# A gathered convolution, two mixtures of experts and attention in one kernel: the gather's start split in two, its edge products in column tiles, and attention's side work moved between the score steps

## The chip, the cores and the metric

The kernel runs on one core of one Trainium2 chip. The metric is the time of one execution on the device in microseconds (us). The kernel before was timed three times, and one further execution was taken with the hardware profiler. Engines are named as the profile names them: PE is TensorE (PEld its weight loads), DVE is VectorE, ACT is ScalarE, POOL is GpSimd, and SP is SyncE, which here only issues DMAs.

## What is computed

The input is 8 sequences of 256 tokens with 128 channels. Two layers follow one another, each a mixing stage and a mixture of 8 experts.

```python
# layer 0, mixing: a convolution whose taps are gathered at computed positions
wave = (x @ wave_w.T + wave_b).reshape(B, L, 8, 2)
freq = 1 + sigmoid(wave[..., 0]) * 15
phase = tanh(wave[..., 1]) * freq
offs = phase[..., None] + freq[..., None] * (arange(32) - 15.5)
pos = clip(arange(L)[None, :, None, None] + offs, 0, L - 1)
gathered = g0 + (pos - floor(pos)) * (g1 - g0)     # rows floor(pos), floor(pos) + 1
kmat = (x @ kernel_w.T).reshape(B, L, 8, 64)       # 64 bins of weights per token and head
w = take_along_axis(kmat, bins(offs), axis=3)
y = einsum('blhs,blhsd->blhd', w, gathered) @ out_w.T
# layer 0, experts: layernorm, top 2 of 8, gelu(x w1 + b1) w2 + b2, then @ expm(g0) expm(g1) expm(g2),
#   mixed with a dense gelu branch through a sigmoid gate
# layer 1, mixing: attention with 16 heads of 8 channels, softmax over 256 keys, then a projection
# layer 1, experts: layernorm, top 2 of 8, (silu(x W1) * (x W2)) W3
```

## The kernel before

It is a hand-ordered program in four stages that end at a barrier each: gather, experts of layer 0, attention, experts of layer 1. In each stage every engine has one list of instructions written out in order, and semaphores carry the data between the lists. An engine takes its instructions strictly in that order, so one that waits holds back all behind it.

**Gather.** The tokens are cut into `NT` = 16 tiles of 128. PE first makes the wave projection of all tiles, from which DVE and ACT make the parameters `par` of every token and head (`FR`, `INV`, `CC`). Each tile then passes through `positions` (ACT, eight activations over 328 grid points), `fractions` (DVE: `whole_tap`, `rest` and the two small pieces of `edge`), `ramps` (ACT), `weighted` (DVE: `rest`, `edge`, `summed`), `turned` and `edges_turned` (PE transposes into `tp_all` and `CF`), `transposed` (ACT copies them to `AT` and `cfS`), `gathered` (PE: products into `yps`, from `AT` with the differenced rows `xn`, and the edge products `YC` from `cfS` with the coarse rows `xc`), `mixed` (ACT, `yS`), `out_rows` (PE) and `output` (ACT). The differenced rows `xn` = `AT` - `xn` are made once, by POOL. The kernels of a tile (`projected` on PE, `kernels` on DVE, two operations on POOL) are stored to DRAM (`store`) and loaded back skewed by nine DMAs (`load`), all issued by SP. The product of three matrix exponentials is a serial chain of 27 steps (`chained` on PE, `chain_step` on DVE), unrelated to the tiles. The first `EARLY` = 4 steps and kernels stand ahead of the tiles, the others are placed between the tiles' operations by `between`:

```python
def step_at(n, place):
    i = EARLY + 3 * n + place - (place > 1)
    return i if place != 1 and i < CHAIN else None
def kernel_at(n, place):
    return n + EARLY if place == 1 and n + EARLY < NT else None
```

So a tile carries three chain steps: one at place 0, which DVE meets in the middle of `fractions(n + 1)` and PE ahead of `turned(n - 1)`, and two at places 2 and 3, close together at the end of `weighted(n)`; PE does the place 3 step just ahead of `gathered(n - 1)`, and the next place 0 step just behind it.

**Attention.** There are 10 rounds for 8 sequences. In round `i`, scores of sequence `i` are made in eight steps of two heads (`scores`: four matmuls into `s_ps`, and in the same step four of the transposed scores `st_ps` of sequence `i - 1`). DVE reduces `s_ps` to row maxima (`largest`, two reductions a step), ACT takes the exponentials of `st_ps` (`powers`, two a step), and the next step on PE waits for both. Everything else is side work between the steps: `project` (PE), `high` (ACT) and `split` (DVE) make queries and keys, `value_rows` the values, `negated` (DVE), `maxima` (PE) and `add_maxima` (DVE) put the maxima into the queries, `values` (PE) and `outputs` (ACT) multiply with the values, `by_token` (PE) and `averaged` (DVE) divide, and two transposes `ot`, a copy `oT` on ACT and two matmuls `pj` on PE project and add to `xs_all` on DVE. The side work shares three PSUM banks `x_ps`. POOL rounds the last stage's weights (two CASTs at L1196, two subtractions at L1200) beside round 0.

## Time and profile before

| | us |
|---|---|
| median of 3 runs | 907.07 (905.65 to 907.98) |
| the profiled execution's own time | 901.43 |
| its span | 899.6 |
| busy: PE / DVE / ACT / POOL | 732.4 / 683.8 / 500.6 / 114.9 |
| gather stage, to | 281.4 |
| experts of layer 0, to | 523.5 |
| attention, to | 733.5 |
| experts of layer 1, to | 899.6 |

The profiled execution lies 5.6 us below the median of the unprofiled runs, and 1.8 us of it lie around the span. A busy share is an average over four stages of which each has another limit, so the stages are read one by one.

### The profile page before, as it was taken

To read this page: it belongs to the slowest core of one execution; us is meant where nothing else is said; L and a number is where in the kernel's file an instruction comes from. 1 tells how busy PE (TensorE), PEld (TensorE's weight loads), DVE (VectorE), ACT (ScalarE), POOL (GpSimd) and SP (SyncE) were. 2 spreads that over 40 slices of the span, in tenths; PEclk is the share of its full clock that TensorE was granted. 3 is DMA by queue.
4 is the path that set the end of the run, shared out by engine and by line. 5 is a ranking of instruction groups with operands and counts; after the bars stand their busy time and mean duration, and the time that the engine had idled before them with its cause. 6 is when DMAs were issued, how large, how long until landed. Compare 5 with 4: busy or idle time off the path is not lost. (4 is left out here: it accounts for less than half of the span.)

```text
span 899.6 us, 14269 instructions
## 1 busy us (share of the span) xinstructions
PE 732.4 (81%) x5162; PEld 588.5 (65%) x5162; DVE 683.8 (76%) x1457; ACT 500.6 (56%) x924; POOL 114.9 (13%) x92
## 2 busy tenths in 40 slices
PE   6258778778676889999999854787877759999996
PEld 5148768767675667877778643444444438888886
DVE  2987978999962798988979858777777527677775
ACT  2765756886643675767857632666666543233232
POOL 0321221223002371000000054000000000000000
PEclk9656866876686989999989966889888869999999
DMA  6543334344222420202002040000000000000000
GB/s 202 162 126 92 95 96 101 111 118 132 67 63 77 141 71 1 94 1 95 0 5 91 1 141 0 2 1 1 2 1 1 1 1 1 1 13 1 12 13 12
DMA packets 76697, 48.27 MB, mean 54 GB/s; under 512 B 54994, under 2 KB 64980, under 8 KB 76628
## 3 DMA queue, kind: packets, MB, share of 16 engines
q1 hardware_dynamic: 73268, 44.75, 17.2%
q10 hardware_dynamic: 3360, 2.62, 1.0%
q8 instruction: 41, 0.67, 0.3%
q14 instruction: 28, 0.23, 0.1%
HBM read 37.85 MB, written 9.50 MB: 53 GB/s over the span
## 5 line engine op out<-in xcount | busy, mean ns | idle before, releaser
L891 ACT ACTIVATE hT<-hps,b1s 128x512 f32<-128x512 f32 x128 | 87.9, 691 | 61.6 <-PE hps L802 61.2
L1057 DVE TENSOR_TENSOR hl<-hT,hh 128x512 fp32r<-128x512 f32 x128 | 94.7, 763 | 24.4 <-ACT hh L897 23.1
L1474 DVE TENSOR_REDUCE mx<-s_ps 128x2 f32<-128x512 f32 x128 | 82.3, 685 | 30.7 <-PE s_ps L1236 30.5
L1409 ACT ACTIVATE pt<-st_ps 128x512 f32<-128x512 f32 x128 | 69.7, 599 | 63.2 <-PE st_ps L1246 62.6
L1672 ACT ACTIVATE act_h<-up 128x512 f32<-128x512 f32 x64 | 38.3, 598 | 89.7 <-PE up L1625 89.7
L306 ACT ACTIVATE tap<-cst_s,par 128x328 f32<-128x328 f32 x128 | 72.3, 652 | 1.3 <-DVE par L601 1.3
L313 ACT ACTIVATE rest<-rest,par 128x264 f32<-128x264 f32 x128 | 53.7, 504 | 25.0 <-DVE rest L547 24.8
L1756 DVE TENSOR_TENSOR hid<-act_h,up 128x512 f32<-128x512 f32 x64 | 43.3, 684 | 28.2 <-PE up L1625 17.3
L1636 PEld LDWEIGHTS eo<-wc,hid 128*128 128x128 f32 x512 | 61.7, 192 | 2.3
L1636 PE MATMUL eo<-wc,hid 128*128 128x128 f32 x512 | 62.1, 275 | 0.0
L897 ACT CAST hh<-hT 128x512 fp32r<-128x512 f32 x96 | 59.3, 618 | 0.0
L802 PE MATMUL hps<-xnh,w1h 128*128 128x512 f32 x128 | 54.7, 427 | 3.5 <-POOL w2l L726 3.5
L1236 PE MATMUL s_ps<-kf,qf 32*128 32x256 f32 x256 | 36.9, 369 | 24.8 <-DVE mx L1474 22.0
L416 PE MATMUL tp_all<-ident,summed 128*128 128x128 f32 x256 | 54.0, 399 | 0.2 <-DVE edge L583 0.2
L802 PE MATMUL hps<-xnh,w1l 128*128 128x512 f32 x128 | 53.1, 415 | 0.0
L802 PE MATMUL hps<-xnl,w1h 128*128 128x512 f32 x128 | 53.1, 415 | 0.0
L416 PEld LDWEIGHTS tp_all<-ident,summed 128*128 128x128 f32 x256 | 52.0, 224 | 0.3 <-DVE edge L583 0.3
L813 PE MATMUL eo<-hh,w2h 128*128 128x512 f32 x128 | 51.5, 402 | 0.4 <-DVE hl L1057 0.4
L1236 PEld LDWEIGHTS s_ps<-kf,qf 32*128 32x128 f32 x256 | 22.7, 215 | 43.0 <-issue 21.8
L813 PE MATMUL eo<-hl,w2h 128*128 128x512 f32 x128 | 50.5, 395 | 0.0
L813 PE MATMUL eo<-hh,w2l 128*128 128x512 f32 x128 | 50.5, 395 | 0.0
L444 PE MATMUL yps<-cfS,xc 128*128 128x32 f32 x256 | 49.5, 362 | 0.0
(252 smaller groups left out, 1734.6 us busy)
## 6 DMA issues: line engine op xcount, KB each, us to landing
kd<-kst SPq DMA_DIRECT2D x16, 512.0 KB, 2.7
xc<-in_x_coarse SPq DMA_DIRECT2D x16, 512.0 KB, 4.0
wdB<-wdd SPq DMA_DIRECT2D x32, 256.0 KB, 5.6
dW<-kd SPq DMA_DIRECT2D x16, 256.0 KB, 3.5
Ks<-kd SPq DMA_DIRECT2D x64, 33.0 KB, 2.1
dW<-kd SPq DMA_DIRECT2D x64, 32.0 KB, 2.1
w1r<-in_w ACTq DMA_DIRECT2D x5, 256.0 KB, 2.8
w2r<-in_w ACTq DMA_DIRECT2D x5, 256.0 KB, 3.2
```

The lines of the kernel that those rows point to most:

```text
L306: last = nc.scalar.activation(tap[n % 2][:, h, :], cst_s[:], ACT.Relu, bias=par[:, CC, n, h:h + 1], scale=par[:, INV, n, h:h + 1])
L313: last = nc.scalar.activation(rest[n % 2][:, h, :], rest[n % 2][:, h, :], ACT.Relu, bias=1.0, scale=par[:, FR, n, h:h + 1])
L416: last = nc.tensor.transpose(tp[k][:, j * P:(j + 1) * P], summed[n % 2][:, h, first + jc * P:first + (jc + 1) * P], ident[:])
L802: last = nc.tensor.matmul(hps[:, k, :], w[e][0][:, k * P:(k + 1) * P], x[q % 2][:], start=(i == 0), stop=(i == 2))
L813: last = nc.tensor.matmul(eo[:, s % 2, :], w[e][1][:, k, :], x[s % 2][:, k, :], start=(k == 0 and i == 0), stop=(k == 3 and i == 2))
L891: nc.scalar.activation(hT[k][:], hps[:, k, :], ACT.Gelu, bias=b1s[:, m:m + 1]).then_inc(h_done, 1)
L897: nc.scalar.copy(hh[s % 2][:, k, :], hT[k][:]).then_inc(hh_done, 1)
L1057: nc.vector.tensor_tensor(hl[s % 2][:, k, :], hT[k][:], hh[s % 2][:, k, :].bitcast(F32), ALU.subtract).then_inc(hl_done, 1)
L1236: last = nc.tensor.matmul(s_ps[k][:, t * L:(t + 1) * L], qf[sb_ % 3][rows, h // 4, t * P:(t + 1) * P], kf[sb_ % 3][rows, h // 4, :], start ...
L1409: nc.scalar.activation(pt[h % 8][:].rearrange("p t q -> p (t q)"), st_ps[k][:], ACT.Exp, scale=SCALE)\
L1474: nc.vector.tensor_reduce(mx[:, :, h:h + 1], s_ps[k][:].rearrange("p (t k) -> p t k", t=2), AX, ALU.max).then_inc(s_used, 1)
L1636: last = nc.tensor.matmul(eo[:, s % 2, t * C:(t + 1) * C], hid[s % 2][:, k, t * P:(t + 1) * P], wc[:, e, k, :], start=(k == 0), stop=(k == 1))
```

## The change

1. **The gather's start.** The wave projection and the parameters are made in two parts, first for tiles 0 and 1 (`LEAD` = 2) as soon as the first half of `XT` is loaded, then for tiles 2 to 15. The grid `cst_s` is loaded earlier, with a semaphore of its own. `EARLY` goes from 4 to 2: two chain steps and two kernels move from the front into the tiles, and a tile's kernel is made two tiles ahead instead of four; on SP `store(n + 1)` now stands behind `load(n)` and `coarse_rows(n - 1)`. The differenced rows are made by DVE ahead of `fractions(0)`, no longer by POOL.
2. **Edge products.** `YC` is made by 16 matmuls of 32 weight columns each in four column tiles, which take only the two heads of their 32 output channels, instead of 8 accumulating ones of 128 columns.
3. **Attention.** The side work of each round is put at other score steps on PE, ACT and DVE, with other banks. The second half of a sequence's queries and keys is projected in the first two steps of its own round, not in the round before, and the addition to `xs_all` moves to the next round's first step.

VectorE's list at the start of the gather stage, before: the last two early kernels (`kst`) and chain steps (`Rk`), then `fractions(0)`.
```order
L497 TENSOR_TENSOR kst<-yps,kb_s 128x8x64
L504 SCALAR_TENSOR_TENSOR Rk<-turn,gs 128x384
L497 TENSOR_TENSOR kst<-kps,kb_s 128x8x64
L504 SCALAR_TENSOR_TENSOR Rk<-turn,gs 128x384
L542 TENSOR_SCALAR edge<-tap 128x512
L544 TENSOR_SCALAR edge<-tap 128x256
L546 TENSOR_SCALAR whole_tap<-tap 128x2112
L547 SCALAR_TENSOR_TENSOR rest<-whole_tap,tap 128x2112
L551 TENSOR_SCALAR edge<-edge 128x512
```
The same place in the changed kernel, behind the second of two early kernels and chain steps.
```order
L511 TENSOR_TENSOR kst<-kps,kb_s 128x8x64
L518 SCALAR_TENSOR_TENSOR Rk<-turn,gs 128x384
L627 TENSOR_TENSOR xn<-AT,xn 128x2048
L556 TENSOR_SCALAR edge<-tap 128x512
L558 TENSOR_SCALAR edge<-tap 128x256
L560 TENSOR_SCALAR whole_tap<-tap 128x2112
L561 SCALAR_TENSOR_TENSOR rest<-whole_tap,tap 128x2112
L565 TENSOR_SCALAR edge<-edge 128x512
L566 TENSOR_SCALAR edge<-edge 128x256
L603 TENSOR_TENSOR wave<-ops,kb_s 128x224
L556 TENSOR_SCALAR edge<-tap 128x512
L558 TENSOR_SCALAR edge<-tap 128x256
```
The subtraction into `xn` now stands ahead of `fractions(0)`, and the wave rows of tiles 2 to 15 between the first two tiles; their parameters follow `fractions(1)`, behind these rows.

VectorE's list at the start of attention, before: `split` (`kf`, `qf`), reductions (`mx`) and the negated maxima (`mxx`).
```order
L1463 SCALAR_TENSOR_TENSOR kf<-x_ps,bqk,hi 128x256 x2
L1463 SCALAR_TENSOR_TENSOR qf<-x_ps,bqk,hi 128x256 x2
L1463 SCALAR_TENSOR_TENSOR kf<-x_ps,bqk,hi 128x256 x2
L1463 SCALAR_TENSOR_TENSOR qf<-x_ps,bqk,hi 128x256 x2
L1474 TENSOR_REDUCE mx<-s_ps 128x2 x6
L1463 SCALAR_TENSOR_TENSOR kf<-x_ps,bqk,hi 128x256 x2
L1474 TENSOR_REDUCE mx<-s_ps 128x2 x2
L1484 TENSOR_SCALAR mxx<-mx 128x2x8
L1485 SCALAR_TENSOR_TENSOR mxx<-mx,mxx 128x2x8
```
The same place in the changed kernel.
```order
L1481 SCALAR_TENSOR_TENSOR kf<-x_ps,bqk,hi 128x256 x2
L1481 SCALAR_TENSOR_TENSOR qf<-x_ps,bqk,hi 128x256 x2
L1492 TENSOR_REDUCE mx<-s_ps 128x2 x4
L1481 SCALAR_TENSOR_TENSOR kf<-x_ps,bqk,hi 128x256 x2
L1492 TENSOR_REDUCE mx<-s_ps 128x2 x2
L1481 SCALAR_TENSOR_TENSOR qf<-x_ps,bqk,hi 128x256 x2
L1492 TENSOR_REDUCE mx<-s_ps 128x2 x2
L1502 TENSOR_SCALAR mxx<-mx 128x2x8
L1503 SCALAR_TENSOR_TENSOR mxx<-mx,mxx 128x2x8
```
Two of the four splits now stand behind the reductions of steps 1 and 2; the negated maxima stand behind step 3 as before.

TensorE's list at the end of a full round, from the projection ahead of score step 6 on, before: the transposes of `o`, `values` (`o_ps`), `project` (`wqk`) and the output projection (`pw`) in one gap.
```order
L1206 MATMUL x_ps<-sT,wqk 128x256 x2
L1236 MATMUL s_ps<-kf,qf 128x256 x2
L1246 MATMUL st_ps<-qf,kf 128x256 x2
L1236 MATMUL s_ps<-kf,qf 128x256 x2
L1246 MATMUL st_ps<-qf,kf 128x256 x2
L1366 MATMUL x_ps<-ident,o 128x128 x2
L1264 MATMUL o_ps<-pt,va 32x256 x8
L1206 MATMUL x_ps<-sT,wqk 128x256 x2
L1377 MATMUL x_ps<-pw,oT 128x128 x2
L1236 MATMUL s_ps<-kf,qf 128x256 x2
L1246 MATMUL st_ps<-qf,kf 128x256 x2
```
The changed kernel, from the second half of score step 6 on.
```order
L1263 MATMUL s_ps<-kf,qf 128x256 x2
L1273 MATMUL st_ps<-qf,kf 128x256 x2
L1233 MATMUL x_ps<-sT,wqk 128x256 x2
L1263 MATMUL s_ps<-kf,qf 128x256 x2
L1273 MATMUL st_ps<-qf,kf 128x256 x2
L1263 MATMUL s_ps<-kf,qf 128x256 x2
L1273 MATMUL st_ps<-qf,kf 128x256 x2
L1389 MATMUL x_ps<-ident,o 128x128 x2
L1291 MATMUL o_ps<-pt,va 32x256 x8
L1397 MATMUL x_ps<-pw,oT 128x128 x2
L1263 MATMUL s_ps<-kf,qf 128x256 x2
L1273 MATMUL st_ps<-qf,kf 128x256 x2
```
`project` has gone from that gap to the one ahead of it, and the rest of the gap stands behind the round's last score step.

The diff, cut to its core (in the parts on attention only added lines and their surroundings are shown; the removed ones stand in the functions above):

```diff
...
-EARLY = 4
+EARLY = 2
+LEAD = 2
...
-    for q in range(4):
+    for q in range(2):
         sp.dma_start(XT[:, q * CH:(q + 1) * CH], x_T[:, q * CH:(q + 1) * CH]).then_inc(ld_x, 16)
+    sp.dma_start(cst_s[:], cst).then_inc(ld_cst, 16)
+    for q in range(2, 4):
+        sp.dma_start(XT[:, q * CH:(q + 1) * CH], x_T[:, q * CH:(q + 1) * CH]).then_inc(ld_x2, 16)
     for m in range(6):
         sp.dma_start(gs[:, m, :], gens[m]).then_inc(ld_g, 16)
...
     coarse_rows(0)
     for n in range(2, NT):
-        if n + 2 < NT:
-            store(n + 2)
         load(n)
         coarse_rows(n - 1)
+        if n + 1 < NT:
+            store(n + 1)
     coarse_rows(NT - 1)
...
         nc.gpsimd.tensor_copy(k[:, :, 2 * BINS - 1:], k[:, :, BINS - 1:BINS]).then_inc(k_out, 1)
-        if n == EARLY - 1:
-            pool.wait_ge(ld_rest, 80)
-            nc.gpsimd.tensor_tensor(xn[:], AT[:], xn[:], ALU.subtract).then_inc(dx_set, 1)
...
-    act.wait_ge(wave_set, 1)
-    nc.scalar.activation(par[:, FR], wave[:, :, 0:H0], ACT.Sigmoid).then_inc(act_done, 1)
-    nc.scalar.activation(par[:, TMP], wave[:, :, H0:], ACT.Tanh).then_inc(act_done, 1)
-    act.wait_ge(ld_rest, 80)
+    def shaped(part, first, end):
+        act.wait_ge(wave_set, part + 1)
+        nc.scalar.activation(par[:, FR, first:end], wave[:, first:end, 0:H0], ACT.Sigmoid).then_inc(act_done, 1)
+        nc.scalar.activation(par[:, TMP, first:end], wave[:, first:end, H0:], ACT.Tanh).then_inc(act_done, 1)
+    shaped(0, 0, LEAD)
+    act.wait_ge(ld_cst, 16)
+    act.wait_ge(par_set, 1)
+    positions(0)
+    positions(1)
+    shaped(1, LEAD, NT)
+    ramps(0)
+    act.wait_ge(ld_rest, 64)
     for j in range(2):
         last = nc.scalar.activation(owh[:, j, :], ow[:], ACT.Copy, scale=own_rows[:, j:j + 1])
     last.then_inc(owh_set, 1)
-    act.wait_ge(par_set, 1)
-    positions(0)
-    positions(1)
-    ramps(0)
+    act.wait_ge(par_set, 2)
     for n in range(NT):
         if n + 2 < NT:
             positions(n + 2)
...
         for b in range(GB):
-            for g in range(2):
-                last = nc.tensor.matmul(YC[:, b * A32:(b + 1) * A32], xc[n % 2][:, g, b, :],
-                                        cfS[:, g, b * A32:(b + 1) * A32], start=(g == 0), stop=(g == 1))
+            toks = slice(b * A32, (b + 1) * A32)
+            for q in range(4):
+                rows = slice(32 * q, 32 * q + 32)
+                last = nc.tensor.matmul(YC[rows, toks], xc[n % 2][:, q // 2, b, rows], cfS[:, q // 2, toks],
+                                        start=True, stop=True, tile_position=(0, 32 * q))
         last.then_inc(y_ready, 1)
     def out_rows(n):
         if n >= 1:
             pe.wait_ge(o_used, n)
+        else:
+            pe.wait_ge(owh_set, 1)
         nc.tensor.matmul(OUT0, ident[:], columns(n), start=True, stop=False)
         pe.wait_ge(ys_ready, n + 1)
         for j in range(2):
             nc.tensor.matmul(OUT0, owh[:, j, :], yS[:, j, :], start=False, stop=False)
         nc.tensor.matmul(OUT0, ow[:], yS[:, 2, :], start=False, stop=True).then_inc(o_ready, 1)
+    def waves(dst, first, end):
+        for n in range(first, end):
+            last = nc.tensor.matmul(dst[:, n * 2 * H0:(n + 1) * 2 * H0], columns(n), kw_s[:, NK:],
+                                    start=True, stop=True)
+        last.then_inc(wave_mm, 1)
     pe.wait_ge(ld_first, 32)
-    pe.wait_ge(ld_x, 64)
-    for n in range(NT):
-        last = nc.tensor.matmul(wps[:, n * 2 * H0:(n + 1) * 2 * H0], columns(n), kw_s[:, NK:],
-                                start=True, stop=True)
-    last.then_inc(wave_mm, 1)
-    pe.wait_ge(ld_g, 112)
+    pe.wait_ge(ld_x, 32)
+    waves(tp[0], 0, LEAD)
     for i in range(EARLY):
         if i >= 2:
             pe.wait_ge(k_half, i - 1)
         projected(i, kps[i % 2][:])
+        pe.wait_ge(ld_g, 112)
         chained(i, 0)
-    pe.wait_ge(owh_set, 1)
+    pe.wait_ge(ld_x2, 32)
+    waves(wps, LEAD, NT)
     for n in range(NT):
         between(n, 0)
...
-    v.wait_ge(wave_mm, 1)
-    nc.vector.tensor_tensor(wave[:], wps[:, 0:NT * 2 * H0].rearrange("p (n w) -> p n w", n=NT),
-                            bc(kb_s[:, NK:], 1, NT), ALU.add).then_inc(wave_set, 1)
+    def wave_rows(part, src, first, end):
+        v.wait_ge(wave_mm, part + 1)
+        nc.vector.tensor_tensor(wave[:, first:end],
+                                src[:, first * 2 * H0:end * 2 * H0].rearrange("p (n w) -> p n w", n=end - first),
+                                bc(kb_s[:, NK:], 1, end - first), ALU.add).then_inc(wave_set, 1)
+    def parameters(part, first, end):
+        v.wait_ge(act_done, 2 * part + 2)
+        G = lambda k: par[:, k, first:end].rearrange("p n h -> p (n h)")
+        link(nc.vector.tensor_scalar(G(FR), G(FR), 15.0, 1.0, ALU.mult, ALU.add))
+        link(nc.vector.tensor_tensor(G(TMP), G(TMP), G(FR), ALU.mult))
+        nc.vector.reciprocal(G(INV), G(FR))
+        link(nc.vector.scalar_tensor_tensor(G(O0), G(FR), -(TAPS // 2 - 0.5), G(TMP), ALU.mult, ALU.add))
+        nc.vector.scalar_tensor_tensor(G(CC), G(O0), -1.0, G(INV), ALU.mult, ALU.mult).then_inc(par_set, 1)
+    wave_rows(0, tp[0], 0, LEAD)
+    parameters(0, 0, LEAD)
     v.wait_ge(ld_g, 112)
     nc.vector.tensor_scalar(x2d(gs, 0, 6), x2d(gs, 0, 6), 2.0 ** -SQUARINGS, None, ALU.mult)\
         .then_inc(gens_set, 1)
...
-    v.wait_ge(act_done, 2)
...
     for i in range(EARLY):
         kernels(i, kps[i % 2][:])
         chain_step(i)
+    v.wait_ge(ld_rest, 64)
+    nc.vector.tensor_tensor(xn[:], AT[:], xn[:], ALU.subtract).then_inc(dx_set, 1)
     fractions(0)
-    for n in range(NT):
+    wave_rows(1, wps, LEAD, NT)
+    fractions(1)
+    parameters(1, LEAD, NT)
+    weighted(0)
+    for n in range(1, NT):
         if n + 1 < NT:
             fractions(n + 1)
...
-return (1, 2, 0, 1)[n] if n < 4 else (n + 1) % 2
+return 1 if n == 0 else (2, 2, 0, 1)[n % 4]
...
 project(0, 0, 0, 2)
 pe.wait_ge(row_used, 1)
...
+value_rows(0, 0)
 for i in range(ROUNDS):
     scores(i, 0)
     values(i - 2, 3)
...
+    if i in whole:
         if i >= 3:
             pe.wait_ge(oT_done, i - 2)
         elif i >= 1:
             pe.wait_ge(max_added, 2 * i - 1)
         else:
             pe.wait_ge(v_used, 1)
...
+        project(i, 1, 1, 0)
+    scores(i, 1)
+    if i in whole:
+        if i >= 3:
+            pe.wait_ge(pj_used, i - 2)
+        elif i >= 1:
+            pe.wait_ge(v_used, i + 1)
+        else:
+            pe.wait_ge(proj_used, 1)
+        project(i, 0, 1, 1)
+    scores(i, 2)
+    values(i - 1, 0)
+    if i - 1 in whole:
+        if i in whole:
+            pe.wait_ge(proj_used, 4 * i + 2)
+        maxima(i - 1, 1, 2)
     scores(i, 3)
     if i - 2 in whole:
...
+        if i in whole:
+            pe.wait_ge(proj_used, 4 * i + 3)
         else:
...
+            pe.wait_ge(oT_done, i - 2)
         by_token(i - 2, 0, 0)
...
+        if i in whole:
+            pe.wait_ge(proj_used, 4 * i + 4)
         else:
             pe.wait_ge(pj_used, i - 2)
         by_token(i - 2, 1, 1)
     scores(i, 4)
...
+    if i + 1 in whole:
+        if i >= 1:
+            pe.wait_ge(max_added, 2 * i)
+        else:
+            pe.wait_ge(proj_used, 2)
+        project(i + 1, 1, 0, 2)
     if i in whole:
...
         if i >= 2:
             pe.wait_ge(o_ready, 2 * (i - 2) + 1)
...
         else:
...
+            pe.wait_ge(proj_used, 4 * i + 3)
+        maxima(i, 0, 0)
     scores(i, 5)
+    values(i - 1, 1)
     if i + 1 in whole:
         if i >= 2:
             pe.wait_ge(o_ready, 2 * (i - 2) + 2)
         else:
...
+            pe.wait_ge(proj_used, 4 * i + 4)
+        value_rows(i + 1, 1)
     scores(i, 6)
+    if i + 1 in whole:
+        pe.wait_ge(proj_used, 4 * i + 5)
+        project(i + 1, 0, 0, 2)
+    scores(i, 7)
     if i - 2 in whole:
         pe.wait_ge(o_ready, 2 * (i - 2) + 2)
         if i in whole:
             pe.wait_ge(max_added, 2 * i + 1)
...
         for t in range(2):
...
+            last = nc.tensor.transpose(x_ps[0][:, t * P:(t + 1) * P], o[:, t, :], ident[:])
         last.then_inc(ot_ready, 1)
     values(i - 1, 2)
...
     if i - 2 in whole:
         if i + 1 in whole:
...
+            pe.wait_ge(v_used, i + 2)
         pe.wait_ge(oT_done, i - 1)
         for t in range(2):
             last = nc.tensor.matmul(x_ps[1][:, t * C:(t + 1) * C], oT[:, t * P:(t + 1) * P], pw[:],
                                     start=True, stop=True)
         last.then_inc(pj_ready, 1)
...
 high(0, 1, 0)
 high(1, 0, 0)
...
+value_rows(0, 0)
 for i in range(ROUNDS):
     powers(i - 1, 0)
+    if i in whole:
+        high(4 * i + 2, 1, 1)
     powers(i - 1, 1)
     outputs(i - 2, 1)
+    if i in whole:
+        high(4 * i + 3, 0, 1)
     powers(i - 1, 2)
+    powers(i - 1, 3)
+    powers(i - 1, 4)
     if i + 1 in whole:
         high(4 * i + 4, 1, 0)
...
     powers(i - 1, 5)
     if i + 1 in whole:
...
+        value_rows(i + 1, 1)
     outputs(i - 1, 0)
     powers(i - 1, 6)
     if i + 1 in whole:
...
+        high(4 * i + 5, 0, 0)
     if i - 2 in whole:
         act.wait_ge(ot_ready, i - 1)
...
+        nc.scalar.copy(oT[:], x_ps[0][:, 0:L]).then_inc(oT_done, 1)
     powers(i - 1, 7)
...
                                 bc(den[:, t, :], 2, HD), ALU.mult).then_inc(o_ready, 1)
+def projected(b):
+    if b not in whole:
+        return
...
+    v.wait_ge(pj_ready, b + 1)
+    x2 = xs_all[:, 2 * b:2 * b + 2, :]
+    nc.vector.tensor_tensor(x2, x_ps[1][:, 0:2 * C].rearrange("p (t c) -> p t c", t=2), x2, ALU.add)\
+        .then_inc(pj_used, 1)
...
 split(0, 1, 0)
 split(1, 0, 0)
...
 for i in range(ROUNDS):
     largest(i, 0)
+    projected(i - 3)
     largest(i, 1)
...
+    if i in whole:
+        split(4 * i + 2, 1, 1)
     largest(i, 2)
+    if i in whole:
+        split(4 * i + 3, 0, 1)
+    largest(i, 3)
+    add_maxima(i - 1, 1, 2)
+    negated(i, 0)
+    largest(i, 4)
+    averaged(i - 2)
+    largest(i, 5)
     if i + 1 in whole:
         split(4 * i + 4, 1, 0)
...
+    largest(i, 6)
+    add_maxima(i, 0, 0)
+    largest(i, 7)
     if i + 1 in whole:
         split(4 * i + 5, 0, 0)
...
     negated(i, 1)
+projected(B - 1)
...
```

## Rows read from the trace of the kernel before

**Rows 1.** gather's start: start us, us, engine, line, tile, shape [idle <-releaser]
```profile
17.47 0.69 ACT L344 ACTIVATE owh<-ow,own_rows 128x128 f32<-128x128 f32 x2 [0.31 <-DMA AT<-in_x_prev]
...
26.85 4.65 POOL L289 TENSOR_TENSOR xn<-AT,xn 128x2048 f32<-128x2048 f32 x1
27.06 5.57 DVE L546 TENSOR_SCALAR whole_tap<-tap 128x2112 f32<-128x2112 f32 x1
...
35.59 0.43 DVE L542 TENSOR_SCALAR edge<-tap 128x512 f32<-128x512 f32 x1
...
40.92 2.36 DVE L561 SCALAR_TENSOR_TENSOR rest<-whole_tap,rest 128x2112 f32<-128x2112 f32 x1
```

**Rows 2.** timeline, first chain step of tiles 2 and 6 on VectorE
```profile
73.37 0.55 DVE L511 SCALAR_TENSOR_TENSOR Y<-Y,turn 128x384 f32<-128x384 f32 x1 [2.10 <-PE turn L386]
...
140.46 0.55 DVE L511 SCALAR_TENSOR_TENSOR Y<-Y,turn 128x384 f32<-128x384 f32 x1 [1.73 <-PE turn L386]
```

**Rows 3.** timeline around the end of tile 5's turn on TensorE
```profile
116.61 1.94 PE L437 MATMUL yps<-AT,xn 128*32 128x64 f32 x64
116.72 0.56 DVE L511 SCALAR_TENSOR_TENSOR Y<-Y,turn 128x384 f32<-128x384 f32 x1 [1.37 <-PE turn L386]
...
118.48 3.62 PE L444 MATMUL yps<-cfS,xc 128*128 128x32 f32 x16
```

**Rows 4.** timeline, end of the gather stage
```profile
254.80 1.10 PE L437 MATMUL yps<-AT,xn 128*32 128x64 f32 x64 [2.46 <-ACT cfS L325]
...
255.83 2.40 PE L444 MATMUL yps<-cfS,xc 128*128 128x32 f32 x16
...
258.04 3.19 PE L416 MATMUL tp_all<-ident,summed 128*128 128x128 f32 x16
...
261.81 0.17 DVE L583 TENSOR_TENSOR edge<-edge,ends 128x8 f32<-128x8 f32 x1
...
280.96 0.39 ACT L336 COPY sT<-ops 128x128 f32<-128x128 f32 x1 [1.74 <-PE ops L455]
```

**Rows 5.** timeline, round 0 of attention
```profile
533.92 1.28 DVE L1474 TENSOR_REDUCE mx<-s_ps 128x2 f32<-128x512 f32 x2
...
540.20 4.49 POOL L1200 TENSOR_TENSOR wal<-wa,wah 128x2048 fp32r<-128x2048 f32 x1
541.46 3.27 DVE L1484 TENSOR_SCALAR mxx<-mx 128x16 fp32r<-128x16 f32 x1
...
544.76 4.42 DVE L1485 SCALAR_TENSOR_TENSOR mxx<-mx,mxx 128x16 f32<-128x16 f32 x1
...
559.74 1.28 DVE L1474 TENSOR_REDUCE mx<-s_ps 128x2 f32<-128x512 f32 x2
```

**Rows 6.** four rounds: window, length, busy us of engines, granted clock, DMA
```profile
559.74:581.49 21.75, 16.77 (x156) 9.85 (x156) 15.42 (x32) 13.72 (x28) 0.00 (x0) 0.84 0.00 1
...
625.84:648.66 22.82, 19.44 (x170) 11.67 (x170) 16.48 (x36) 13.80 (x28) 0.00 (x0) 0.80 0.01 2
648.66:670.21 21.55, 16.91 (x178) 10.10 (x170) 16.38 (x36) 13.50 (x28) 0.00 (x0) 0.98 0.00 1
...
693.04:710.64 17.60, 12.47 (x142) 7.07 (x138) 13.04 (x28) 8.85 (x18) 0.00 (x0) 0.87 0.01 2
```

**Rows 7.** VectorE in round 5: count | busy, mean ns | idle before <-releaser
```profile
L1474 DVE TENSOR_REDUCE mx<-s_ps 128x2 f32<-128x512 f32 x16 | 10.3, 685 | 2.9 <-PE s_ps L1236 2.9
L1463 DVE SCALAR_TENSOR_TENSOR kf<-x_ps,bqk,hi 128x256 fp32r<-128x256 f32 x4 | 1.8, 480 | 1.1 <-ACT hi L1391 1.1
L1463 DVE SCALAR_TENSOR_TENSOR qf<-x_ps,bqk,hi 128x256 fp32r<-128x256 f32 x4 | 1.8, 480 | 1.0 <-ACT hi L1391 1.0
```

**Rows 8.** timeline, one score step and its projection in round 3
```profile
615.65 1.13 PE L1206 MATMUL x_ps<-sT,wqk 128*128 128x256 f32 x4
615.74 1.29 DVE L1474 TENSOR_REDUCE mx<-s_ps 128x2 f32<-128x512 f32 x2 [1.09 <-PE s_ps L1236]
...
616.78 1.02 ACT L1391 ACTIVATE hi<-x_ps,lo_bias,lo_row 128x256 fp32r<-128x256 f32 x2
```

More of the change, by code:

```diff
@@ L1299, in _ @@
                 values(i - 2, 3)
-                if i - 1 in whole:
-                    if i in whole:
-                        pe.wait_ge(proj_used, 4 * i + 4)
-                    else:
-                        pe.wait_ge(o_ready, 2 * (i - 3) + 2)
-                    maxima(i - 1, 1, 0)
-                scores(i, 1)
-                if i + 1 in whole:
-                    if i >= 3:
-                        pe.wait_ge(pj_used, i - 2)
-                    else:
-                        pe.wait_ge(proj_used, 4 * i + 3 + (i == 0))
-                    project(i + 1, 1, 0, 1)
-                scores(i, 2)
-                values(i - 1, 0)
-                if i + 1 in whole:
+                if i in whole:
                     if i >= 3:
```

80 lines of the change are left out of this document (5 added, 75 removed).

## The prediction

> **What bounds the kernel now.** The table of stages came first: the two expert stages are not touched, so only the gather stage and attention can move, the others shift with them. Then came the timeline of the gather's start, VectorE's waits and the timeline of the stage's end, and for attention the busy time by rounds and VectorE's groups in one undisturbed round.
>
> In the gather VectorE does `fractions` and `weighted` of tile after tile almost without a gap, so the stage's end is set by when it starts, by its waits, and by what PE and ACT still have to do behind it. The start: the last load that ACT waited for, `AT`, was in at 17.47; `weighted(0)` began at 40.92, and on the way stands one DVE operation of 5.57 that began while POOL subtracted `xn` and ended 1.1 after it [rows 1]. The waits: at place 0 of the chain VectorE waits for PE, 2.10 at tile 2, the same at two later tiles, and 1.73 at tile 6, 8.0 in four waits [rows 2]. Its cause is in the next group: PE does the gathered products (1.94) and the edge products (3.62) between the place 3 step and the next place 0 step [rows 3]. The end: VectorE is through at 262.0, the last output is written at 281.35, and `gathered` of tiles 13, 14 and 15 stand one behind the other between these times: 1.10 and 2.40 each, then the next tile's transposes [rows 4].
>
> In attention a round of 21.55 holds 16 reductions and little else that is long on VectorE; it waits 2.9 for scores and 2.1 for ACT's `hi` [rows 7]. The waits come from bunching: a projection (1.13) and `hi` (1.02) follow the step they are put behind, and `split` waits for them [rows 8]. Round 0 is longer than any: the negated maxima take 3.27 and 4.42, each to the end of a POOL subtraction of 4.49, and the reductions of round 1 start only at 559.74 [rows 5].
>
> **The gather's start.** DVE's first long operation now has only three things ahead: the small parameters of two tiles, two kernels with chain steps, and `AT`. `AT` keeps its place in SP's list, so it lands at 17.5; the two kernels and steps should be done by then, since nothing of them needs more than the generators, which are loaded ahead. The subtraction has 2048 columns and two SBUF inputs, like L561's 2112 in 2.36 [rows 1]: 2.3, to 19.8. `fractions(1)` takes 5.33 from 35.59 to 40.92 with a chain step of 0.55 [rows 1, 2]; `fractions(0)` the same without it, 4.8, to 24.6, `fractions(1)` to 29.9. The wave rows and five operations on 112 columns cost below 0.55 each (that is 384 columns), at most 3.3, at least 6 x 0.17 (the 8-column L583 of [rows 4]); I take 2.4, to 32.3. So `weighted(0)` starts 8.6 earlier. ACT keeps up: 16 activations of `positions` in about 9 from 10 on, `ramps(0)` behind the second parameters' first half, done by 30. POOL is out of the way, so the 5.57 is not repeated. **What takes the cover away:** kernels are now made two tiles ahead. SP stores tile n + 1 behind `load(n)`, and `load(n + 1)` waits for it; I put the way from VectorE's kernel over POOL, the store and nine issues to the landed loads at about 16 (an estimate: each of these waits was hidden before, so no row bounds it well), against two tiles of some 13 between them. That slack of 10 hides it; if the way took over 26, every tile would wait for the rest.
>
> **Moved into the tiles.** Two chain steps (0.55 each), two kernels (512 columns, 0.7 each) and one more pair of steps at places 2 and 3, whose second waits 1.37 [rows 3]: +3.9.
>
> **The edge products.** The trace before has no such matmul. The nearest row is L437, whose 64 instructions of 32 weight columns take 1.10, and 1.94 at the lower clock [rows 3, 4]. The 32 new ones then cost 0.55 and 0.97. Bounds: 0.3 (they stream 32 columns, not 64), and 4.8, twice as many instructions at the old price. I take 0.55, by the row that shares the form. In the tail this saves 1.85 three times: 5.6. At place 0 it takes 2.65 from PE's way at the lower clock, more than the longest wait, so all 8.0 go.
> The Trainium skill (TensorE: Matmul & The Clock Gate, LDWEIGHTS) has a weight load's time go with its columns alone: 32 loads of 32 are half of 16 of 128, which would make it 1.2. The sum by it would be 2.0 worse in the tail and some 1 at place 0. L437's row speaks for the lower figure.
>
> Gather: -8.6 - 8.0 + 3.9 - 5.6 = -18.3.
>
> **Attention, full rounds (2 to 6).** I walked the new lists through one round with this round's durations: a score step holds PE 0.44, its reductions can start after 0.54 and take 1.29, the next step follows, 1.88 if nothing else intervenes. The eight steps come out as 2.4 (`values` and `project` on PE), 2.2 (ACT: `high` ahead of the exponentials), 2.4 (the same), 2.5 (`add_maxima` of the round before must end before step 4), 2.9 (PE's `maxima` behind VectorE's averages), 2.1, 2.1, and 2.7 (the split that the next round's step 0 needs): 19.3. VectorE's waits in it are 3.4, its own work is unchanged. At the lower clock a round costs more: 22.82 at a granted clock of 0.80 against 21.55 at 0.98 [rows 6]. With PE's gaps fuller I double that cost in half of the rounds: 20.5 on the mean against 22.3, -1.8 in each of five, -9.0.
>
> **Round 1** has no `by_token`, averages or output projection: 16.8 by the same walk, 18.1 with 1.3 for the clock, against 21.75 [rows 6]: -3.6. **Round 7** now carries two projections that stood in round 6: 18.6 against 17.60 [rows 6], +1.0. **The drain** behind it keeps its length: its steps go at ACT's pace.
>
> **Round 0.** Two splits no longer stand ahead of the first reductions: they start at 532.6, not 533.92 [rows 5]. Each of steps 1 to 3 takes 2.0, and the negated maxima come at 539.8 to 540.1, before POOL's first subtraction at 540.20 [rows 5]. Then only the second of the two is caught, to 544.8, not 549.2. From there 8.5 to the reductions of round 1 (before 10.6, as a kernel and two projections less wait in it): 553.3 against 559.74, -6.4. If the first is caught too, -2.1. The margin is 0.1 to 0.4, so I give the first 6 in 10.
> The Trainium skill (SBUF — State Buffer, two separate sides) has GpSimd and such VectorE operations take turns on one port pair, whole instructions at a time; the trace agrees (3.27 and 4.42, both ending with POOL's).
>
> Attention: -6.4 - 3.6 - 9.0 + 1.0 = -18.0.
>
> **Sum.** -36.3 against the profiled execution's 901.43 gives 865.1. The median of the runs stands 5.6 above it: 871.
>
> **Rivals.**
> - *POOL catches both negated maxima*: +4.3, 875. It belongs to the forecast's case, as does any small slip; together 0.55, 865 to 879.
> - *Attention's rounds keep most of their waits*: ACT has 13.5 busy in 21.55 [rows 6] and gets `high` ahead of the exponentials twice, so a new wait on it may replace the old. Rounds 2 to 6 then bring 2, not 9: 878. For it speaks ACT's order, against it that VectorE waits for ACT 2.1 now. 0.15.
> - *The edge products are dear, or the tail runs at 1.2 GHz* because PE does less: at 1.94 + 0.97 for 1.10 + 0.55 and dearer transposes, 2 a tile, 6 in the tail: 877. 0.10.
> - *The start doesn't do what it says*: kernels or skewed loads arrive no earlier, and `weighted(0)` gains nothing: +8.6, 880. The loads before were issued behind kernels at 20 to 25, and these now come while `xn` and `AT` are still landing. 0.07.
> - *Better than reckoned* (no clock cost in rounds): 860. 0.05.
> - *No change*: both gains are off the path or eaten. 0.03.
> - *Slower*: PE has 16.91 busy in a round at 2.4 GHz, and 2.5 more with the clock at 0.80 [rows 6]; at 1.2 GHz throughout it is about 24. If the fuller gaps kept it there, the projections that now stand in every second gap would make PE the bound at 26.5 a round. That is 4.2 more in seven rounds, 29, less the gather's 18: 918. It decides from a mean round of 24.9 on. Nothing in the rows shows such a stretch. 0.05.
>
> **Range and chances.** 860 to 888 takes in the forecast's case, the next three and most of the fifth, and the bounds of the edge products (0.3 to about 2). A measurement of this kernel tells about 0.3% from no change, 2.7 us. Faster 0.92, within it 0.03, slower 0.05.
>
> **What would show it.** Right: DVE's L627 starts near 17.5 and `weighted(0)` (L575) near 32; L452 takes about 0.55 for 32 instructions; no wait above 0.5 for PE at place 0; gather over near 263; rounds of 19.3 to 21. Wrong: L575 of tile 0 waiting on a DMA of `Ks` or `dW`; L1502 of 3 or more; DVE waits for `s_ps` or `hi` that sum to 5 a round; a granted clock below 0.8 over attention.

## The result, and the profile after

The changed kernel takes 878.81 us, median of 4 runs (875.44 to 882.84), against 907.11 for the kernel before beside it (905.65 to 907.98): a ratio of 0.9692, 95% interval 0.9654 to 0.973. That is 28.3 us less. The forecast was 871, with a range of 860 to 888. The profiled execution took 877.47 with a span of 875.7; the gain from profile to profile is 23.9 of the 36.3 that the sum gave.

The gather's start, VectorE's timeline (columns as in [rows 1]):

```profile
18.01 2.29 DVE L627 TENSOR_TENSOR xn<-AT,xn 128x2048 f32<-128x2048 f32 x1 [1.04 <-DMA AT<-in_x_prev]
...
32.47 2.35 DVE L575 SCALAR_TENSOR_TENSOR rest<-whole_tap,rest 128x2112 f32<-128x2112 f32 x1
```

The difference waits for `AT` and takes 2.29, and `weighted(0)` begins at 32.47, where [rows 1] have 40.92. VectorE's waits in the gather, in us, times and the longest:

```profile
DVE Y L525 <- PE turn L392: 6.9, 5, 1.4
```

Before, these were 13.4 in ten, with 2.10 the longest [rows 2]. The five that are left are place 3's, 1.35 to 1.38 each, like the 1.37 of [rows 3]; none is at place 0. The end of the stage, timeline:

```profile
258.77 1.10 PE L443 MATMUL yps<-AT,xn 128*32 128x64 f32 x64 [2.45 <-ACT cfS L325]
259.69 0.48 PE L452 MATMUL yps<-cfS,xc 128*32 128x32 f32 x32
...
263.11 1.09 PE L769 MATMUL aux<-ident,sT 128*128 128x128 f32 x4 [0.73 <-PEq L109]
...
264.24 0.89 DVE L977 BATCH_NORM_STATS2 stats<-aux 128x6 f32<-128x128 f32 x4 [15.05 <-PE aux L769]
```

The gathered products still take 1.10, the edge products 0.48 instead of 2.40 [rows 4]. The next stage's PE work starts at 263.11. Round 0 of attention, the answer to [rows 5]:

```profile
521.08 1.90 POOL L1223 CAST wbh<-wb 128x2048 fp32r<-128x2048 f32 x1
523.06 4.55 POOL L1227 TENSOR_TENSOR wal<-wa,wah 128x2048 fp32r<-128x2048 f32 x1
...
522.61 0.41 DVE L1502 TENSOR_SCALAR mxx<-mx 128x16 fp32r<-128x16 f32 x1
523.05 0.19 DVE L1503 SCALAR_TENSOR_TENSOR mxx<-mx,mxx 128x16 f32<-128x16 f32 x1
```

Both negated maxima slip in ahead of POOL's subtraction, the second by 0.01. Now attention by rounds, from the first reductions (round 0) to the end of the drain, columns as in [rows 6]:

```profile
515.26:533.12 17.86, 11.03 (x60) 7.31 (x60) 14.73 (x29) 5.74 (x10) 13.71 (x5) 0.81 0.18 51
533.12:554.17 21.05, 17.30 (x148) 10.55 (x144) 15.20 (x30) 13.09 (x26) 0.00 (x0) 0.76 0.00 1
554.17:573.79 19.62, 16.12 (x178) 9.93 (x174) 15.96 (x34) 13.80 (x28) 0.00 (x0) 1.00 0.01 2
573.79:593.42 19.63, 16.13 (x178) 9.94 (x174) 16.31 (x36) 13.80 (x28) 0.00 (x0) 1.00 0.00 1
593.42:616.11 22.69, 19.77 (x170) 11.77 (x166) 16.29 (x35) 13.94 (x28) 0.00 (x0) 0.77 0.00 1
616.11:637.75 21.64, 18.03 (x181) 10.84 (x179) 16.30 (x36) 13.80 (x28) 0.00 (x0) 0.92 0.01 2
637.75:660.45 22.70, 19.79 (x169) 11.78 (x166) 16.30 (x35) 13.94 (x28) 0.00 (x0) 0.77 0.00 1
660.45:680.56 20.11, 14.58 (x157) 8.17 (x155) 14.81 (x32) 11.51 (x23) 0.00 (x0) 0.90 0.01 1
680.56:709.84 29.28, 22.55 (x152) 12.31 (x148) 3.98 (x14) 11.26 (x23) 0.00 (x0) 0.62 0.00 1
```

Two things stand out. A full round takes 19.6 at a granted clock of 1.00 and 22.7 at 0.77. And the last row, the drain (the two rounds at the end that have no scores of their own to reduce), is 29.28 long at 0.62. The same stretch of the kernel before:

```profile
710.74:733.55 22.81, 16.01 (x140) 9.50 (x132) 3.55 (x12) 10.77 (x22) 0.00 (x0) 0.81 0.00 1
```

That is 6.5 us that the forecast did not have. What such a drain looks like in the changed kernel's timeline:

```profile
684.33 0.79 PE L1273 MATMUL st_ps<-qf,kf 32*128 32x256 f32 x4
685.15 1.08 ACT L1428 ACTIVATE pt<-st_ps 128x512 f32<-128x512 f32 x2 [1.50 <-PE st_ps L1273]
...
687.01 1.93 PE L1291 MATMUL o_ps<-pt,va 128*32 128x256 f32 x16
```

At full clock the same two PE groups take 0.50 and 1.07 (`all_three`, below). ACT's exponentials, which should set the pace, wait 1.50 for PE's transposed scores.

### The profile page after: what moved, and what is told of

Its sections match the earlier page's. It is cut to its first block and busy times, and to the rows that moved or that the text cites. A ratio compares the mean times of both kernels' runs of the same rounds, so it can differ in the third digit from the quotient of the medians.

```text
span 875.7 us, 14793 instructions
## 1 busy us (share of the span) xinstructions
PE 697.6 (80%) x5418; PEld 549.5 (63%) x5418; DVE 670.6 (77%) x1464; ACT 501.6 (57%) x926; POOL 114.5 (13%) x91
## 5 line engine op out<-in xcount | busy, mean ns | idle before, releaser
L1084 DVE TENSOR_TENSOR hl<-hT,hh 128x512 fp32r<-128x512 f32 x128 | 91.7, 738 | 29.6 <-ACT hh L924 28.0
L443 PE MATMUL yps<-AT,xn 128*32 128x64 f32 x1024 | 28.0, 293 | 35.1 <-ACT cfS L325 35.1
L422 PE MATMUL tp_all<-ident,summed 128*128 128x128 f32 x256 | 44.7, 348 | 6.2 <-DVE edge L597 6.2
L443 PEld LDWEIGHTS yps<-AT,xn 128*32 128x32 f32 x1024 | 24.5, 159 | 38.5 <-ACT cfS L325 36.9
```

Source lines behind the costliest of these rows:

```text
L1084: nc.vector.tensor_tensor(hl[s % 2][:, k, :], hT[k][:], hh[s % 2][:, k, :].bitcast(F32), ALU.subtract).then_inc(hl_done, 1)
```

## The experiments

All ratios are to the kernel before in the same call. "Drain" is the stretch of the last row above. `g_only`, `y_only`, `a_only` and `sub_first` ran together, so did `gy`, `d_old`, `f_drain` and `f_rounds`, and so did `again`, `pool_wait`, `f_busy` and `all_three`. Of these groups only the last has the changed kernel in it (`again`), so for the others "against the changed kernel" compares two ratios to the kernel before.

**The parts alone.** `g_only` is the kernel before with all of the gather's edits except the edge products. Against the changed kernel's gather that is:

```diff
-                        toks = slice(b * A32, (b + 1) * A32)
-                        for q in range(4):
...
+                        for g in range(2):
+                            last = nc.tensor.matmul(YC[:, b * A32:(b + 1) * A32], xc[n % 2][:, g, b, :],
```

> The kernel before with the new start of the gather alone (two parts of waves and parameters, the difference on VectorE, two tiles of kernels ahead, the new order of SP's list). The edge products keep their eight accumulating matmuls, attention its old order. Parts add up: start -8.6, moved work +3.9, and the waits for PE at place 0 stay, so the gather stage ends 4 to 5 us earlier, attention as before, the run about 902. Rival, that the earlier start is eaten by PE because the edge products still hold it: gather within 1 us of before, about 906.

Measured: ratio 0.995 (0.9906 to 0.9994). `weighted(0)` starts at 32.51, but the next stage's first statistics come only 2.6 earlier (280.17 against 282.78). VectorE waits for the chain longer than before (13.4 there), and the tail is as long as it was (21.47 from VectorE's last operation to the next statistics, 20.79 before):

```profile
DVE Y L523 <- PE turn L392: 14.9, 11, 2.1
```

`y_only` is the kernel before with the opposite edit, the sixteen 32-column matmuls and nothing else.

> The kernel before with the edge products in column tiles alone. My theory: waits of VectorE at place 0 of the chain go (8.0 us in before) and the tail of the gather is 5.6 shorter, so the stage ends 10 to 13.6 earlier and the run is at 894 to 897. L452's counterpart takes 0.5 to 0.6 for a tile at full clock and about 1 at half. Rival by weight columns alone: 1.2 at full clock, tail 3.6 shorter. Rival: the column tiles cost as much as before, run at 907.

Measured: ratio 0.9788 (0.9736 to 0.984), some 19 us by the ratio (13.6 from profile to profile); the gather's end is 16.6 earlier (266.17). The rows on waits, and on the tail at full and, three tiles earlier, at the lower level:

```profile
DVE Y L513 <- PE turn L386: 6.8, 5, 1.4
```

```profile
235.61 0.66 PE L446 MATMUL yps<-cfS,xc 128*32 128x32 f32 x32
...
262.79 0.48 PE L446 MATMUL yps<-cfS,xc 128*32 128x32 f32 x32
...
266.17 0.89 DVE L952 BATCH_NORM_STATS2 stats<-aux 128x6 f32<-128x128 f32 x4 [11.82 <-PE aux L744]
```

So the edge products cost 0.48 at 2.4 GHz and 0.66 at 1.2 GHz, and this one edit is the largest part of the whole change.

`a_only` is the kernel before with `bank_of` and attention's three new lists:

```diff
-            return (1, 2, 0, 1)[n] if n < 4 else (n + 1) % 2
+            return 1 if n == 0 else (2, 2, 0, 1)[n % 4]
```

> The kernel before with attention's new order alone. By the two traces attention of the changed kernel is 6.6 us shorter than before, not 18: round 0 about 9 shorter, rounds 1 to 6 5.5 shorter, round 7 and the drain 8 longer. If that is a property of the order, this run is at 900 to 902 and its drain (from the last reductions' negated maxima to the end) again near 29 us against 22.9, at a granted clock of 0.6. Rival, that the long drain was chance in one profile: drain near 23 and the run at 893 to 895.

Measured: ratio 0.9846 (0.9758 to 0.9933), too wide to tell 7 from 14 us. In its profiled execution the gather, which it does not touch, is 4.8 longer than before, so only the pattern of its rounds is used: full rounds of 19.63, 19.62, 22.70, 21.59, 22.70 and a drain of 29.25.

`gy` is the changed kernel with attention in its old order.

> The gather's two parts together, attention in its old order. If the parts add, the gather ends where it does in the changed kernel (first stats of the next stage near 264) and attention takes what it took before (199.6 us from its first reduction to its end), so the run is 4 to 6 us above the changed kernel, about 883 to 885. Rival, that attention's new order is worth nothing in the median because its drain gives back what the rounds gain: within 2 us of the changed kernel.

Measured: ratio 0.9759 (0.9727 to 0.9791). With the changed kernel at 0.9683 (0.9645 to 0.972, `again` below), attention's new order is worth 0.8% or some 7 us (each ratio is known to about 3 us). Its trace holds the surprise: the rounds are those of before to 0.03 us, and yet the drain, in the **old** order, is 29.0.

```profile
607.65:630.46 22.81, 19.50 (x170) 11.64 (x170) 16.48 (x36) 13.83 (x28) 0.00 (x0) 0.80 0.01 2
630.46:652.03 21.57, 16.82 (x176) 10.08 (x170) 16.39 (x37) 13.52 (x28) 0.00 (x0) 0.97 0.00 1
692.43:721.43 29.00, 22.50 (x140) 12.42 (x132) 3.55 (x11) 10.76 (x22) 0.00 (x0) 0.51 0.00 1
```

**The drain: order or clock.** `d_old`, the changed kernel with PE's old order in rounds 8 and 9 (the one edit of five shown):

```diff
                     project(i, 1, 1, 0)
+                if i == B:
+                    maxima(i - 1, 1, 2)
                 scores(i, 1)
```

> The changed kernel, but the two last rounds (8 and 9, with no scores of their own to reduce) have PE's work in the old order: the second negated maxima are transposed right behind step 0 instead of behind step 2, the values of heads 4 to 7 ahead of step 5, and the output's transposes, values and projection ahead of step 7. Theory A, the order makes the long drain: the drain comes down from 29.3 to about 23 to 25 and the run is 4 to 6 faster. Theory B, the clock makes it (granted 0.5 to 0.6 in the drain, values at 1.94 instead of 1.07): the drain stays at 26 or more while the granted clock in it stays below 0.7.

Measured: ratio 0.9757 (0.9722 to 0.9791), above the changed kernel's, and a drain of 31.87 at the lower level of the clock throughout:

```profile
676.55:708.42 31.87, 25.36 (x152) 14.18 (x148) 3.97 (x12) 11.13 (x23) 0.00 (x0) 0.50 0.00 1
```

So PE's old order alone does not bring the short drain back. As the clock never rose in this one, it does not tell what the order is worth at a higher clock.

`f_drain`, the changed kernel with idle matmuls in round 8 (`idle_work(k, bank)` issues `k` matmuls of `ident` by `ident` into the bank; nothing uses them):

```diff
+                    if tb == B - 1:
+                        if s == 0:
+                            pe.wait_ge(s_used, 16 * B)
+                        idle_work(2, s_ps[0][:, 0:P])
                     if s % 4 == 0:
                         pe.wait_ge(max_added, 2 * tb + s // 4 + 1)
```

> The changed kernel with two matmuls of 128 columns more ahead of each score step of round 8, written into a score bank that nobody reads any more, so that PE has no gaps there. They compute nothing that is used. Theory B, the clock makes the long drain: the granted clock in the drain rises to 0.8 or more and the drain falls from 29.3 to about 24. Theory A, the order makes it: the clock may rise but the drain does not shorten, or it is longer by the added 2.6 to 5 us of PE time.

Measured: ratio 0.9655 (0.9612 to 0.9697), drain 25.30 at 0.90:

```profile
670.17:695.47 25.30, 20.66 (x184) 14.06 (x180) 3.97 (x12) 11.19 (x23) 0.00 (x0) 0.90 0.00 1
```

More work on PE makes the stretch 3.4 to 4.0 shorter than in the changed kernel's two profiles, in the same order. So the clock makes a part of the long drain, as theory B has it, and theory A can't be all of it; whether the order has a share is taken up below. The interval overlaps that of the changed kernel, so of the run's time this alone says little. The profiled execution, 861.4 long, also had a short round 0 (17.95) and short rounds behind it, where its instructions are the changed kernel's.

**The rounds: filling PE's gaps.** `f_rounds`, the changed kernel with ten idle matmuls in each of rounds 1 to 7:

```diff
                     by_token(i - 2, 1, 1)
+                if i in whole and i - 1 in whole:
+                    idle_work(4, o_ps[:, L:L + P])
                 scores(i, 4)
...
                 if i in whole:
+                    if i - 1 in whole:
+                        idle_work(6, o_ps[:, L:L + P])
                     if i >= 2:
                         pe.wait_ge(o_ready, 2 * (i - 2) + 1)
```

> The changed kernel with ten matmuls of 128 columns more in rounds 1 to 7, four while PE waits for the added maxima ahead of step 4 and six while it waits for the averages behind it, into a half bank that is free then. They compute nothing that is used. Theory B: the clock falls behind exactly these gaps (granted 0.5 from 605, 629, 649 and 681 on), so the full rounds that took 22.7 (three of five) come to 19.6 to 20.5 and the run is 5 to 8 us faster. Rival, that the gaps are not what lowers the clock: the 22.7 us rounds stay, and each round is 0 to 1 longer.

Measured: ratio 0.9566 (0.9522 to 0.961), below the changed kernel's interval. Rounds 2 to 6 are 19.85 to 19.87 long, all at 1.00; two of them and the drain:

```profile
603.65:623.51 19.86, 18.14 (x198) 12.34 (x194) 16.30 (x36) 13.80 (x28) 0.00 (x0) 1.00 0.01 2
643.36:663.23 19.87, 18.14 (x198) 12.34 (x194) 16.29 (x35) 13.81 (x28) 0.00 (x0) 1.00 0.01 2
682.06:706.69 24.63, 17.69 (x156) 9.82 (x148) 3.97 (x12) 11.28 (x23) 0.00 (x0) 0.84 0.01 1
```

`f_busy` is the control, the same ten in another place:

```diff
                 values(i - 1, 0)
+                if i in whole and i - 1 in whole:
+                    idle_work(10, o_ps[:, L:L + P])
                 if i - 1 in whole:
```

> Control for the gaps: the changed kernel with the same ten idle matmuls in rounds 1 to 7, but put behind the values of step 2, where PE is busy anyway, and none in the gaps around step 4. If what matters is that the gaps around step 4 are filled, the clock still falls behind them and rounds of 22 to 24 us stay. If the mere amount of PE work in a round matters, the clock stays at full and the rounds are 19.6 plus up to 1.7 for the ten matmuls.

Measured: ratio 0.9771 (0.9732 to 0.981). The clock stays at 1.00 in rounds 2 to 6 here too, but each is 2.0 longer than 19.62 and the run slower than the changed kernel, as PE's extra work now stands on the path:

```profile
630.50:652.12 21.62, 18.33 (x198) 12.18 (x194) 16.30 (x36) 13.80 (x28) 0.00 (x0) 1.00 0.01 2
```

So my reason, that filling just the gaps around step 4 is what matters, falls: ten more matmuls a round held the clock in either place. The place decides only whether they cost 0.24 or 2.0.

**POOL and round 0.** `sub_first` has POOL round, subtract, round, subtract:

```diff
+            for k, (low, high, full) in enumerate(((wal, wah, wa), (wbl, wbh, wb))):
+                nc.gpsimd.tensor_copy(flat2(high[:]), flat2(full[:])).then_inc(ffn1_high, 1)
+                pool.wait_ge(ffn1_high, k + 1)
```

> The changed kernel with POOL's two rounding casts and two subtractions of the experts' weights in the order cast, subtraction, cast, subtraction. The first subtraction then runs about 1.9 us earlier and covers the moment of round 0's negated maxima. Theory, the maxima of round 0 were missed by a hair in the profiled run (0.41 and 0.19 us long, the second begun 0.01 before POOL's subtraction): now one of them lasts until POOL ends, 2.5 to 4.5 us, and round 1 starts 2 to 4 us later, the run 2 to 4 us longer. Rival, contention with POOL costs nothing on this path: both stay below 0.5 and the time does not move.

Measured: round 0 is 22.02 instead of 17.86, by two caught instructions, the one to the end of POOL's subtraction, the other to the end of its rounding:

```profile
519.64 4.50 POOL L1225 TENSOR_TENSOR wal<-wa,wah 128x2048 fp32r<-128x2048 f32 x1
524.09 1.89 POOL L1223 CAST wbh<-wb 128x2048 fp32r<-128x2048 f32 x1
...
521.29 2.89 DVE L1500 TENSOR_SCALAR mxx<-mx 128x16 fp32r<-128x16 f32 x1
524.22 1.81 DVE L1501 SCALAR_TENSOR_TENSOR mxx<-mx,mxx 128x16 f32<-128x16 f32 x1
```

The mechanism is there, yet no longer run shows: ratio 0.9673 (0.9624 to 0.9722). The interval is 4.4 us wide on either side, as much as the 2 to 4 expected, so it does not exclude them.

`again` is the changed kernel itself, beside the last group.

> The changed kernel as it is, once more, beside the three others on the same chip. Its profiled round 0 may come out at 17.9, 22 or 26 us: POOL's subtraction started 0.01 us behind the second negated maximum in one profile, and ahead of the first in two kernels with the same instructions up to there. The median is expected between 875 and 883.

Measured: 877.03 us, ratio 0.9683 (0.9645 to 0.972). The same kernel, and this time both maxima are caught, to POOL's ends:

```profile
522.94 4.50 POOL L1227 TENSOR_TENSOR wal<-wa,wah 128x2048 fp32r<-128x2048 f32 x1
...
523.38 4.11 DVE L1502 TENSOR_SCALAR mxx<-mx 128x16 fp32r<-128x16 f32 x1
527.52 4.42 DVE L1503 SCALAR_TENSOR_TENSOR mxx<-mx,mxx 128x16 f32<-128x16 f32 x1
```

Round 0 is 26.40, 8.5 longer, and the span, 875.1, is 0.6 shorter than the first profile's.

`pool_wait` makes POOL wait:

```diff
             pool.wait_ge(ffn1_in, 64)
+            pool.wait_ge(max_set, 1)
```

> The changed kernel, but POOL's rounding and subtraction of the experts' weights wait until the first pair of round 0's negated maxima is written, so that it can catch neither. Theory: round 0 is then at 17.9 us in every execution, and the median lies 2 to 6 below that of the changed kernel in the same call; POOL's 4.5 us pieces fall between the two pairs of maxima. Rival, that the gain is eaten by a catch elsewhere, because POOL's second piece now ends later and covers the second pair: round 0 at 20 to 22 and no gain.

Measured: ratio 0.9687 (0.9649 to 0.9725) against 0.9683, no gain that these intervals could show. In the trace the rival came out: the second pair is caught (its first instruction takes 2.85), and round 0 is 22.56.

**All three.** `all_three` joins `pool_wait`, `f_rounds` and `f_drain`.

> The changed kernel with POOL waiting for the first negated maxima, the ten idle matmuls around step 4 of rounds 1 to 7, and two ahead of each score step of round 8. If the three gains are independent, round 0 is at 17.9, rounds 2 to 6 at 19.9, the drain at 24 to 25, and the run at 856 to 864, 15 to 22 below the changed kernel. Rival, that the clock's falls only move elsewhere (into the tail of the gather or the experts): above 868.

Measured: 866.99 us, ratio 0.9555 (0.9528 to 0.9583) against 0.9683 for the changed kernel beside it: the fastest with `f_rounds`, from which it can't be told. It is 3 above what I expected at most. In its profile round 0 is 22.00, 4.1 more than hoped, as POOL catches the second pair, and round 2 takes 21.43 at a clock of 0.92; rounds 3 to 6 and the drain hold at full clock. Round 6 and the drain:

```profile
637.64:657.51 19.87, 18.15 (x198) 12.35 (x194) 16.30 (x36) 13.80 (x28) 0.00 (x0) 1.00 0.01 2
676.09:699.33 23.24, 18.60 (x180) 12.44 (x179) 3.98 (x13) 11.20 (x23) 0.00 (x0) 1.00 0.00 1
```

## Why the prediction was right, and where its terms were off

The sum by its own terms, against the kernel before, in the changed kernel's two profiles; all are differences between marks (first statistics behind the gather, attention's first instruction, the second pair of negated maxima of each round, end of the drain):

| term, us | forecast | first profile | `again` |
|---|---|---|---|
| gather | -18.3 | -18.5 | -18.8 |
| experts, layer 0 | 0 | +1.2 | +1.2 |
| up to and with round 0 | -6.4 | -9.4 | -0.9 |
| round 1 | -3.6 | -0.7 | -2.6 |
| rounds 2 to 6 | -9.0 | -5.3 | -11.3 |
| round 7 | +1.0 | +2.5 | +2.1 |
| drain | 0 | +6.5 | +5.9 |
| experts, layer 1 | 0 | -0.2 | -0.1 |
| sum | -36.3 | -23.9 | -24.5 |

So the gather came as forecast, and attention did not: it brought 6.4 and 6.8 of the 18.0. The +1.2 stands in a stage that was not changed; that stage took 239.6 to 245.9 in the profiles of this case, so a difference of this size in one profile is not read. The median lies at the upper edge of the forecast's own case (865 to 879), and beside 878, which the forecast gave to a rival with another reason.

**The gather's start, right.** Forecast `weighted(0)` 8.6 earlier, at 32.3; it is 8.45, at 32.47. POOL is out of the way as reckoned, and the kernels, made two tiles ahead, show no wait on a DMA.

**The edge products, right in kind, priced too high.** The nearest row gave 0.55 and 0.97; measured are 0.48 and 0.66. The 8.0 of place 0 went as forecast. But three of the five waits at place 3, 0.67 to 0.95 before, came to 1.36 to 1.38, so the waits fell from 13.4 to 6.9, by 6.5 and not by 8.0. The Trainium skill (TensorE: Matmul & The Clock Gate, LDWEIGHTS) has a load's time go with its columns. The estimate by it was half of the old price, 1.2 at the higher level of the clock and 1.8 (half of 3.62) at the lower; the trace does not agree at either, and the measurement decides. In `y_only` the tail, from VectorE's last operation to the next statistics, is 9.0 shorter (11.82 against 20.79), not 5.6, and PE also ran it at a granted clock of 1.00 against 0.80. In the changed kernel it is 5.7 shorter (15.05), at 0.75; with the same instructions it was between 12.16 at 1.00 (`gy`) and 16.24 at 0.68 (`f_rounds`), so the gather's end moves by 4 us with the clock. The total of the gather came out because errors cancelled: alone, the start brings 2.6 (forecast 4.7) and the edge products 16.6 (forecast 13.6). In `g_only` the 8.45 is handed back in part, for VectorE waits 1.5 more for the chain and the tail, still PE's, is 0.7 longer.

**Round 0, right in mechanism, decided by PE's clock.** The prediction put the margin at 0.1 to 0.4 and gave the middle case 6 in 10. Six profiles have the same instructions up to the end of round 0. In two neither of the maxima is caught (17.86 and 17.95 in `f_drain`), in four both are (26.40, and 26.51, 25.86 and 26.30 in `d_old`, `f_rounds` and `f_busy`), and the middle case never comes. What differs is the length of the score steps ahead of the maxima, here the second one of the first profile and of `again`:

```profile
516.60 0.51 PE L1263 MATMUL s_ps<-kf,qf 32*128 32x256 f32 x4 [0.32 <-DVE mx L1492]
```

```profile
516.32 0.80 PE L1263 MATMUL s_ps<-kf,qf 32*128 32x256 f32 x4 [0.25 <-DVE mx L1492]
```

Where these scores take 0.51, at full clock, the first negated maximum comes 7.2 to 7.4 behind the first reductions, ahead of POOL; where they take 0.80, at the lower level, it comes 8.4 to 9.0 behind them, under POOL's subtraction. The forecast's time for it (539.8 to 540.1 in the old kernel's count) held at full clock, and it left the other level out. That a caught maximum lasts to the end of POOL's instruction showed in `again`, `sub_first` and `pool_wait`, as the Trainium skill's rule on the shared ports (SBUF — State Buffer, two separate sides) has it.

In the changed kernel's two profiles the 8.5 us make no difference to the span, since rounds 1 to 7 took 147.4 in the first and 139.0 in `again`. But that is no rule: in `f_drain`, whose edit comes later, they took 138.9 behind a round 0 of 17.95, so round 7 ended 156.8 behind the first reductions, and not 165.3 or 165.4.

**Rounds 2 to 6, right at full clock.** The walk gave 19.3 for a round at 2.4 GHz; it is 19.62, and with the clock's cost 20.5. Means over the five rounds are 21.26 and 20.05 in the two profiles, and 20.03 to 20.67 in `sub_first`, `d_old`, `f_drain` and `pool_wait`, which have the same rounds. The cost of the lower clock was to be double that of before, 2.5; it is 3.1 (22.70 against 19.62). My reading, which no run isolates, is that PE's projections now sit between steps where everything waits for them. Round 1 was costed too low: 16.8 by the walk and 1.3 for the clock, where 19.0 to 22.1 were measured at granted clocks of 0.72 to 0.87. No profile has it at 1.00, so whether the walk or the clock was mis-sized stays open.

**The drain, the step that failed.** "Its steps go at ACT's pace" holds only while PE runs at full clock. The old order took 22.8 at a granted clock of 0.81, 25.0 at 0.67 (`y_only`) and 29.0 at 0.51 (`gy`); the new one 23.2 at 1.00 and 25.3 at 0.90 (both with idle matmuls in it), 24.6 at 0.84, 26.2 at 0.76 (`sub_first`), and 28.7 to 30.0 at 0.61 to 0.66. The kernel before and `gy` have the same instructions there, so 6.2 us between them come with the clock alone. But at like clocks the new order is the longer one: 24.6 at 0.84 against 22.8 at 0.81, 28.7 at 0.66 (`again`) against 25.0 at 0.67. By a line through the old order's two lower values it would take 26.2 at 0.62, an estimate. So of the 6.5 us some 3.4 are the clock's, and about 3 come from the order or from where in the drain the clock is low. No run separates these two. A part of it is only a shift of the mark, for more work stands behind it (152 records on PE against 140, ACT 11.26 against 10.77). Round 7 adds 1.5 to its +1.0: its step 4 has lost the projection, and PE is idle there for most of three microseconds (1.12 busy from 671 to 674) as the clock falls (1.00 in the three before, 0.57 in the three behind). What in the change sends the clock down at this place is not settled: `gy` has the same instructions in attention as the kernel before and still falls, to 0.51; `y_only`, with the old order too, falls to 0.67, and `g_only` stays at 0.81. The Trainium skill (TensorE: Matmul & The Clock Gate, Part 1) says that the chip's look at PE's activity runs free of the program, so that the same kernel's slow stretches differ from run to run; the rounds of 22.7 here, which are rounds 4 and 6 in one profile and none in `again`, agree.

**Up to the median.** I added 5.6 for the distance of profile and median. It was 1.3 this time, which hid 4 of the 12 us by which the sum was off: the median came 7.8 above the forecast.
